# A fused attention and FP4 feed-forward block on one core: fill and tail reordered, first h values by pairs

## The reference

```
xn = (x - mean) / sqrt(var + 1e-5)
# attention, 16 heads of 8 channels, 2 codes for each head
q, k, v = split(xn @ w_qkv.T)
q = softmax(q . code * scale) * scale         # over the 2 codes
k_exp = exp(k . code * scale - max over tokens)
kv = cumsum(k_exp * v) / (cumsum(k_exp) + 1e-9)   # along the tokens
attn = (q . kv) @ w_out.T
# feed-forward, 352 wide
# fp4(a): blocks of 16 scaled by max|a| / 6, rounded to {0, .5, 1, 1.5, 2, 3, 4, 6}, scaled back
h = silu(fp4(xn) @ fp4(w_gate).T) * (fp4(xn) @ fp4(w_up).T)
ffn = fp4(h) @ fp4(w_down).T
out = x + attn + ffn
```

## Time and profile before

| | |
|---|---|
| median of 3 runs | 134.34 us |
| profiled execution | 133.35 us |
| its span | 131.6 us |
| instructions in the span | 2409 |
| PE busy | 122.0 us, 93% |
| DVE busy | 119.4 us, 91% |
| POOL busy | 115.4 us, 88% |
| ACT busy | 107.1 us, 81% |
| DMA read and written | 2.90 and 2.10 MB |

### The profile page before, as it was taken

The page is one execution under the profiler, slowest core; times in us unless marked ns, Lnnn a source line. Parts: engine busy times, 40 slices in busy tenths (PEclk is TensorE's granted clock), DMA queues, the critical chain, the costliest instruction groups (busy, mean ns, idle before and its releaser), DMA issues.

```text
span 131.6 us, 2409 instructions
## 1 busy us (share of the span) xinstructions
PE 122.0 (93%) x797; PEld 101.7 (77%) x797; DVE 119.4 (91%) x277; ACT 107.1 (81%) x268; POOL 115.4 (88%) x129
## 2 busy tenths in 40 slices
PE   3998779969999999999999999999999999999990
PEld 3997567546657878988897869669978898999990
DVE  2798799999998999999999999999999999999802
ACT  0457999999999999999999799997868877764430
POOL 5388899768999999999999999999978999999910
PEclk9999999999999999999999999999999999999999
DMA  3993000000000000002000000300002000000422
GB/s 101 274 373 134 0 10 0 2 0 0 0 0 0 0 5 0 0 0 80 5 2 0 2 0 5 144 16 0 0 0 80 5 0 0 0 5 0 159 80 80
DMA packets 3931, 5.14 MB, mean 39 GB/s; under 512 B 528, under 2 KB 1872, under 8 KB 3920
## 3 DMA queue, kind: packets, MB, share of 16 engines
q1 hardware_dynamic: 2832, 4.44, 9.7%
q10 hardware_dynamic: 1088, 0.56, 1.4%
HBM read 2.90 MB, written 2.10 MB: 38 GB/s over the span
## 4 chain that ended last, share of the span: by engine, by line
PE 76%; ACT 17%; POOL 3%; issue 1%; DVE 1%; POOLq 0%; DVEq 0%
PE ps L564 16%; PE ps L503 12%; PE ps L500 11%; PE ps L550 9%; PE ps L604 6%; PE ps L558 5%; PE ps L367 4%; ACT L506 3%; PE ps L457 3%; PE ps L458 3%; ACT silu_sb L506 2%; ACT xn L347 2%; PE ps L412 2%; PE ps L359 2%; PE ps L493 2%; PE ps L389 1%
## 5 line engine op out<-in xcount | busy, mean ns | idle before, releaser
L564 PEld LDWEIGHTS ps<-wd_t,hq_t 128*128 128x128 f32 x192 | 24.1, 192 | 1.8
L564 PE MATMUL ps<-wd_t,hq_t 128*128 128x128 f32 x192 | 25.2, 275 | 0.0
L500 PE MATMUL ps<-wg_t,xq_t 128*128 128x352 f32 x64 | 23.8, 469 | 1.0 <-ACT xq_t L497 0.9
L523 POOL TENSOR_TENSOR yh<-h,h_r 128x704 f32<-128x704 f32 (+1 forms) x20 | 22.9, 1145 | 0.4 <-ACT h_r L520 0.4
L503 PE MATMUL ps<-wu_t,xq_t 128*128 128x352 f32 x64 | 23.0, 466 | 0.3 <-ACT silu_sb L506 0.3
L546 POOL TENSOR_TENSOR hq<-qh,h_max 128x704 f32<-128x704 bf16 (+1 forms) x20 | 22.8, 1144 | 0.5 <-DVE qh L536 0.4
L409 POOL TENSOR_TENSOR kv<-kv 128x288 f32<-128x288 f32 x24 | 19.1, 798 | 1.6 <-DVE kv L404 1.0
L554 ACT ACTIVATE hq_t<-ps 128x384 f32<-128x384 f32 x32 | 15.4, 494 | 4.1 <-PE ps L550 4.0
L452 POOL TENSOR_TENSOR o_codes<-kv,q_n 128x1024 f32<-128x1024 f32 x8 | 15.8, 1969 | 0.7 <-DVE q_n L448 0.7
L509 DVE TENSOR_TENSOR h<-silu_sb,ps 128x352 f32<-128x352 f32 x32 | 15.7, 507 | 0.2 <-PE ps L503 0.2
L500 PEld LDWEIGHTS ps<-wg_t,xq_t 128*128 128x128 f32 x64 | 10.8, 190 | 5.6 <-ACT xq_t L497 1.1
(11 more groups left out here) (113 smaller groups left out, 283.3 us busy)
## 6 DMA issues: line engine op xcount, KB each, us to landing
x_all<-x SPq DMA_DIRECT2D x8, 256.0 KB, 4.8
out<-out_sb SPq DMA_DIRECT2D x8, 256.0 KB, 2.0
w_raw<-w_down ACTq DMA_DIRECT2D x1, 176.0 KB, 4.4
w_raw<-w_up ACTq DMA_DIRECT2D x1, 128.0 KB, 3.1
w_raw<-w_gate SPq DMA_DIRECT2D x1, 128.0 KB, 3.2
wqk_raw<-w_qkv ACTq DMA_DIRECT2D x1, 128.0 KB, 4.4
wqkv_t<-w_qkv ACTq DMA_DIRECT2D x1, 64.0 KB, 4.1
wo_t<-w_out_t SPq DMA_DIRECT2D x1, 64.0 KB, 4.3
```

The lines of the kernel that those rows point to most:

```text
L500: return nc.tensor.matmul(ps[:, k, 0:FF], xq_t[:, b % 2, t * P:(t + 1) * P], wg_t[:, :], start=True, stop=True)
L523: return nc.gpsimd.tensor_tensor(blocks(yh[:, b % 2, ff_span(t, n)], n * HB), h[:, b % 2, h_span(t, n), 0:BLOCK], spread(h_r[:, b % 2, h_s ...
L564: last = nc.tensor.matmul(ps[:, k, t * P:(t + 1) * P], hq_t[:, b % 2, t, c * P:(c + 1) * P], wd_t[:, c * P:(c + 1) * P], start=(first and ...
```

## The change

- PE: 18 unread products instead of 28.
- Batch 0: variance and negative mean on DVE (`variance_dve`, `negative_mean_dve`), tiles 2 and 3 of xn on DVE (`x_normalised_dve`). Batch 1: all four tiles of xn on ACT.
- Weights: up is quantised ahead of gate. Quantisation and transposition of the weights stand earlier in the queues.
- `kv_products_psum` is kept in batches 0 and 7; batches 1 to 6 use `v_evict` and `kv_products`.
- `h_product` over two tiles in batches 0, 2 and 4 (six of them; `silu` stays by tiles). Batch 0 is quantised by pairs. Batch 7 stays by single tiles; its tile 3 is rounded into PSUM and dequantised by DVE (`h_round_psum`, `h_dequant_psum`).
- Tail: the o projection of batch 7 by tiles, tiles 3 and then 2, 0, 1 in banks 1, 5, 4 and 5, each with its own `residual_tile` and `store_tile`. Stores of batches 0 to 5 are issued by twos: 1 and 0 behind the second residual, 3 and 2 behind the fourth, 5 and 4 behind the sixth.
- The order of all five queues and the assignment of banks change throughout. There are 9 preloads and 8 changes to silu, as before.

```diff
+        def variance_dve(a, z):
+            return nc.vector.tensor_scalar(halves(var_eps[:, a:z, :]), moments[:, a:z, :, :, 2], 1.0 / D, LN_EPS, op0=ALU.mult, op1=ALU.add)
+        def x_normalised_dve(b, j0=0, j1=TILES):
+            for j in range(j0, j1):
+                last = nc.vector.tensor_scalar(xn[:, b % 2, j * D:(j + 1) * D], x_all[:, b, j * D:(j + 1) * D], moments[:, b, j // 2, j % 2, 1:2], rstd[:, b, j:j + 1],
+                                               op0=ALU.subtract, op1=ALU.mult)
+            return last
+        def h_dequant_psum(b, t, n, k):
+            return nc.vector.tensor_tensor(by_block(hq[:, b % 2, t:t + n, 0:FF], n), by_block(ps[:, k:k + n, 0:FF], n), h_scales(b, t, n), ALU.mult)
+        def residual_tile(b, t, k):
+            return nc.vector.tensor_tensor(out_sb[:, b % 2, t * P:(t + 1) * P], x_all[:, b, t * P:(t + 1) * P], ps[:, k, t * P:(t + 1) * P], ALU.add)
+        def store_tile(b, t, done):
+            nc.sync.dma_start(out_v[b][:, t * P:(t + 1) * P], out_sb[:, b % 2, t * P:(t + 1) * P]).then_inc(done, 16)
...
             sp.wait_ge(resid_done, 6)
             store(5, stored1)
+            store(4, stored0)
             sp.wait_ge(resid_done, 7)
             store(6, stored0)
             sp.wait_ge(resid_done, 8)
-            store(7, stored1)
+            store_tile(7, 3, stored1)
+            sp.wait_ge(resid_done, 9)
+            store_tile(7, 2, stored1)
+            sp.wait_ge(resid_done, 10)
+            store_tile(7, 0, stored1)
+            sp.wait_ge(resid_done, 11)
+            store_tile(7, 1, stored1)
...
-            pool.wait_ge(vareps_done, 1)
+            pool.wait_ge(varepsd_done, 1)
             pool.wait_ge(pads_done, 1)
             root_power(0, 1).then_inc(rpow_done, 1)
...
-            x_normalised_pool(0, 2, 4).then_inc(xnp_done, 1)
...
-            x_normalised_pool(1).then_inc(xnp_done, 1)
...
+            pool.wait_ge(kexp_done, 2)
+            kv_products(1).then_inc(kvm_done, 1)
...
-            variance(0, 1).then_inc(vareps_done, 1)
-            negative_mean(0, 1).then_inc(negmean_done, 1)
...
+            act.wait_ge(shift_done, 2)
+            x_normalised_act(1).then_inc(xn_done, 1)
```

More of the change, by code:

```diff
@@ L930, in _ @@
[L930 to L934 removed]
+            act.wait_ge(knegmax_done, 2)
+            x_square(1, 3).then_inc(sqx_done, 1)
+            act.wait_ge(xqT_done, 1)
+            xq_evict(0, 7).then_inc(xqev_done, 1)
+            act.wait_ge(xnT_done, 3)
+            x_evict(2, 2).then_inc(xnt_done, 1)
+            act.wait_ge(kshift_done, 2)
@@ new lines, in _ @@
+            act.wait_ge(xqev_done, 2)
+            q_exp(1, 5).then_inc(qexp_done, 1)
+            act.wait_ge(vlog_done, 2)
+            root_guess(4, 8).then_inc(guess_done, 1)
+            act.wait_ge(qkv_done, 3)
+            v_evict(2, 2).then_inc(vev_done, 1)
+            act.wait_ge(gate_done, 7)
+            silu(1, 0, 1, 7).then_inc(silu_done, 1)
+            q_relu(2, 2).then_inc(qrel_done, 1)
+            act.wait_ge(yx_done, 3)
+            act.wait_ge(silu_done, 5)
+            x_square(2, 7).then_inc(sqx_done, 1)
@@ L1015, in _ @@
[L1015 to L1024 removed]
+            silu(2, 3, 1, 4).then_inc(silu_done, 1)
```

2338 lines of the change are left out of this document (1138 added, 1200 removed).

## The result

The changed kernel takes 131.78 us (median of five executions, 131.74 to 133.49), the one before in the same runs 134.34 (133.62 to 134.75). The ratio is 0.986, 95% interval 0.981 to 0.991. Ratios leave out executions that took over 1.5% longer than the fastest of the same kernel. The forecast was 132.5 us, range 130.6 to 134.7, and "faster" at 0.74.

What follows compares the result with a forecast made beforehand. ACT was taken to set the pace from 10.65 to 37.3 us, then PE. 40.0 + 85.3 + 1.7 + 0.1 + 0.27 + 2.46 gave a 129.8 us span, 131.55 by the profile's count; ratio 0.987 on 134.34 made 132.5, range 130.6 to 134.7.

Steps and rivals of the forecast that it cites:

- Unread products: end at 7.6: Start of PE's queue: with 18 unread products instead of 28 they end at 7.6 us, against 10.2.
- ACT's walk: first silu table at 22.7: ACT's queue walked through the fill: first silu table load at 22.7 us against 21.96 before, third log table ending at 34.4.
- PE at 40.0 with 24.5 us of its list done: PE at the fill's end: 24.5 us of its work done at 40.0, against 23.4 at 40.22, so 1.3 us ahead.
- Nothing more than 1.7 us lost after 40: PE after 40 us: it again loses 1.7 us beyond the 85.3 us left of its list.
- DVE: -2.6 us: DVE's work over the whole kernel: 2.6 us less, bounds 1.7 and 3.2, standing on no path of its own.
- Tail: -0.4: Behind PE's last down: a 128-column residual of 0.27 us replaces 0.69, saving 0.4; the store's 2.46 is kept.
- The wait of residual(6): hidden, with 0.8 us to spare: Late on DVE: residual(6) waits for store(4); 3.6 us of DVE operations cover 0.8 for issues and 2.0 for landing.
- From 131.55 to 132.5 by the ratio of median to profile: Last step: 131.55 us, counted like the profiled execution, becomes a 132.5 us median, as the earlier median was 0.7% above its profile.
- A (POOL holds everything): POOL bounds the kernel, so the fill's gain counts nothing and only the tail's does: -0.9 us, 133.4; chance 0.21.
- B: DVE and POOL both give time, with PE's list 2.6 us ahead at 40: -3.0 us, 131.3; chance 0.15.
- C (ACT sets the fill): ACT, given 2.0 us more in the fill, delays batches 2 and 3: +1.2 us, 135.5; chance 0.13.
- D, the clock: PE's clock falls to half in the fill, costing 1.6 us: 134.1; chance 0.03.

Runs made afterwards that it cites:

- early-store version: The changed kernel with store(4) issued as soon as residual(4) is written and store(5) after residual(5): 131.88 us, ratio 0.985.
- one-store kernel: The early-store version with one store of the whole batch 7 after the last residual, in place of per-tile stores: 132.62 us, ratio 0.989.
- the one with more on PE: The early-store version with one gate and one up of batch 4 issued twice on PE: 132.62 us, ratio 0.989.
- 8 unread products: The changed kernel with 8 unread products in place of 18: 132.95 us, ratio 0.992.
- the one without pairs: The early-store version with the six h products over two tiles taken apart into twelve singles: 132.01 us, ratio 0.985.

## Why the prediction was right

The direction and the time held: 132.5 forecast, 131.8 measured. The gain is made where the prediction put it, in PE's lead out of the fill and in the tail, but not in its amounts. From the profile before to an undisturbed one after, the span falls by 1.5 us (131.6 to 130.1). PE's last `down` comes 0.56 earlier, where 1.35 was forecast, and what follows it is 0.94 shorter, where 0.4 was. That the two misses nearly cancel (span 129.8 forecast, 130.1 measured) is luck. The medians are 2.56 apart, so about 1 us of the gain is in neither step. And the fill's part hangs on the unread products: with 28 of them the new order is slower than the old one.

Taken by its own steps, with the profile of the early-store version (span 130.1, like the four undisturbed executions of the changed kernel) for the times that the low clock shifts:

- **Unread products: end at 7.6.** 7.81 to 9.38 in the profiles with 18. The prediction let the pace step from 0.218 us to 0.111 at 5.00, as in the profile of before. Where the step comes there (the one-store kernel and the one with more on PE) they end at 7.8, near the forecast; in the others it comes later, up to 8.3. It read the granted clock of 1.00 in both stretches as the full level; but twice the pace is what the two levels differ by, and the column has no record there (see 8 unread products). Windows of the unread products alone (a record that lies across an edge counts in both windows, so 6 or 7 are 0.218 us apart and 11 or 12 are 0.111 apart), in the second run of the changed kernel and in the one-store version:

```profile
5.00:6.00 1.00, 1.00 (x7) 1.00 (x7) 1.00 1.03 348
6.00:7.00 1.00, 1.00 (x6) 1.00 (x6) 1.00 1.07 385
7.00:8.00 1.00, 1.00 (x7) 1.00 (x6) 1.00 1.09 362
```

```profile
5.00:6.00 1.00, 1.00 (x11) 1.00 (x11) 1.00 0.77 250
```

  The first three lines are of the second run of the changed kernel, the last of the one-store version. The slow pace ends at 5 us in one execution and at 8 in another. The end of the unread products moves by 1.5 us with it.
- **Statistics on DVE.** 0.12 each forecast, 0.17 and 0.16 with their overlap; power at 4.86, not 4.65; xn on DVE 0.60 for two tiles against 0.50. Right within 0.2.
- **ACT's walk: first silu table at 22.7.** Too late: 20.80 to 21.81 in the undisturbed profiles (the 22.91 of the profile after is the clock). The third log table ends at 32.85 (31.57 + 1.28), not 34.4. But the walk stopped at 36.5, and the chain shows ACT as the bound up to 42.03. The 1.5 us that ACT is ahead of the walk bought nothing for PE.
- **PE at 40.0 with 24.5 us of its list done.** `gate(2,0)`, the last of those, ends at 40.17 in the early-store version: 1.15 ahead of the kernel before, against 1.3 forecast. Right, though the way there was not.
- **Nothing more than 1.7 us lost after 40.** 127.79 - 40.17 = 87.6, against 85.3 of list: 2.3 lost. The extra 0.6 lies before 42.03: of the 1.87 us between the two, PE's work by its prices is 1.26.
- **POOL unchanged in sum, `o_products(0)` at 29.3 to 30.** 29.97, and 115.6 us.
- **DVE: -2.6 us.** Wrong in the busy time: 119.6 against 119.4. Its parts were right, as the durations by group add up: `kv_products_psum` -2.7, h products -0.8 (pairs at 0.88), the other passes over h -1.0, statistics, xn, dequantisation and residuals +2.0, together -2.5. All other groups add 0.5, so the durations fall by 2.0 (139.2 to 137.1). What gave it back is overlap: neighbours that run into each other count once in the busy time, and they do so for 2.2 us less than before. Why, no run shows. It did not matter for the sum, in which DVE stood at nothing; but at 68 us 0.93 of 1.19 us added on DVE reached the end, so DVE is not as idle a bystander as the sum has it.
- **Tail: -0.4.** Mis-sized. From the last `down` to the end of the span are 2.31 us (127.79 to 130.1) against 3.25 (128.35 to 131.6): -0.94. 0.4 of it is the residual, as forecast; 0.5 is the store, for which I kept 2.46 where a tile takes 2.0. The run with one store puts that term at 0.5. POOL's side was 5.0, not 4.7.
- **The wait of residual(6): hidden, with 0.8 us to spare.** This step failed, in three of five profiles. The cover was right: 2.8 us by the forecast (0.8 and 2.0), and 2.8 in each of the three profiles with a wait (4.34 - 1.55, 4.03 - 1.24, 3.65 - 0.86). The landing was not: the step took the median, 2.0 us. Behind another store it is 2.3, which is still hidden, as 2.8 just is; in the three in which a load of instructions holds it up it is 3.7, 4.0 or 4.3, and residual(6) waits 0.86 to 1.55. "The excess goes straight to the end" held: 1.2 us for 1.55 of wait.
- **Sum: span 129.8.** 130.0 to 130.1: fill and middle +0.7, tail -0.5.
- **From 131.55 to 132.5 by the ratio of median to profile.** This cost the forecast most. Its own sum was 131.55, the changed kernel's median is 131.78. The profile of before has a span of 131.6, and of some 50 executions of that kernel none is below 131.5; its median is 0.7% above because most are slower in something that its profile doesn't hold. A later end of the slow pace is such a thing, and 28 products are exposed to it more than 18: argued from the windows above, as only one trace of before exists. The changed kernel's typical execution is its undisturbed one, so for it the scaling added 1 us that wasn't there.

Of the rivals, A (POOL holds everything) was half true: POOL is a bound near 57 us, but the fill's gain arrived. B needed PE 2.6 ahead at 40, and it was 1.15. C (ACT sets the fill) had the mechanism and the wrong price: ACT does bind, to 42 us, and PE was as far as forecast. D, the clock, at 0.03 was about right for the median and too low for single executions: 2 of 11 of the changed kernel have 0.987 and take 1.6 us more, the price forecast.

## What to carry to other kernels

A store whose landing frees a buffer should be issued as soon as its data are ready: moved up, store(4) got some 9 us more of cover for one more wait on SP. A margin worked out from the median landing isn't one: here 2.0 us is the median, 2.3 the rule behind another store, and 4.3 came when a load of instructions met the transfer. To find what bounds a middle stretch in which several engines are full, add a microsecond to each in turn and read the distance between two fixed points: the chain named PE alone, and DVE and POOL turned out to be worth as much at that place. An edit that only helps together with another (here the new order and the cut of the unread products) is worth trying each way: in the old order the cut gave 1.0 us in three of twelve executions, in the new one its absence costs 3.0. Before scaling a sum from one profiled execution to a median, ask whether that execution is typical of its kernel; this one was among the fastest of its kind.

## What the runs showed of the hardware

- The pace of the first products changes from 0.22 us a record to 0.11 at some point between 5 and 8.3 us, from run to run, while the clock column says 1.00 throughout. The trace's clock records begin only with that step (at 5.1 us in the one-store kernel, 8.3 in the one without pairs), three profiles have none, and without a record the column says 1.00. It doesn't tell this start; the durations do.
- A mean granted clock of 0.987 means one stretch at the half clock (from 12.3 to 15.7 us in the profile after), and mostly 1.0 to 2.0 us of time; in the kernel with 8 products the one execution with it took no longer than the others. 0.975 in the kernel before with 18 products costs about 3 us.
- PE busy 0.66 and 0.28 of two microseconds (15 to 17 us before) brought no fall of the clock, 0.40 and 0.53 at the same place with 18 products did. What ahead of that decides stayed open.
- A 256 KB store lands in 2.0 us alone and in 2.3 right behind another one. In four profiles a load of 16 KB of instructions falls on such a pair or comes at its end, and the second lands in 2.8, 3.7, 4.0 or 4.3 us; in two of them the first is late as well, 3.4 and 3.8. A 64 KB store lands in 1.6 us, and in 2.8 with such a load.
